# A perceiver layer's tail: one root for two norms, causal values straight to rows of queries, ranks from logits, other fillers

## What is computed

```python
def ffn(x):                         # x is layernorm(x2), eps 1e-5
    h = x + attention(rmsnorm(x, attn_norm_w), wq, wk, wv, wo)   # 16 heads of 16, rotary, causal
    return h + moe_ffn(rmsnorm(h, ffn_norm_w), router_w, w1, w2, w3)
def rmsnorm(x, w):
    return w * (x / sqrt(mean(x * x) + 1e-6))
def moe_ffn(x):                     # softmax, the best 2 of 8, renormalized
    topv, topi = top_k(softmax(x @ router_w), 2)
    combine = sum(topv / sum(topv) * one_hot(topi, 8))
    ye = (silu(x @ w1[e]) * (x @ w3[e])) @ w2[e]     # w1, w3: 256 x 512, w2: 512 x 256
    return sum over e of combine[e] * ye
out = x2 + ffn(layernorm(x2))
```

## Time and profile before

| | us |
|---|---|
| median of 3 runs | 535.7 (535.12 to 536.69) |
| the profiled execution | 535.16 |
| its span | 533.4 |
| PE busy in the span | 504.4 |
| DVE, ACT, POOL busy | 386.6, 346.4, 90.0 |

### The profile page before, as it was taken

How to read it: one execution, slowest core, us unless ns; L and a number is a source line. 1 busy time by engine, 2 the same in 40 slices (tenths; PEclk the granted TensorE clock), 3 DMA queues, 4 the chain that set the end, 5 groups by cost and what they waited for, 6 DMA issues and landing times.

```text
span 533.4 us, 19592 instructions
## 1 busy us (share of the span) xinstructions
PE 504.4 (95%) x8408; PEld 459.6 (86%) x8408; DVE 386.6 (72%) x712; ACT 346.4 (65%) x688; POOL 90.0 (17%) x75
## 2 busy tenths in 40 slices
PE   7898999999999999999999999999989989775997
PEld 7888899999999999999999999999877878564886
DVE  5488877777877777787787877787774347938574
ACT  3422687787778878878788787877766720162663
POOL 6761101111111110110110111110000000052000
PEclk9999999999999999999999999999999999869899
DMA  6554544343344434434434344432380079900000
GB/s 200 163 170 150 162 146 140 121 141 125 123 156 148 133 126 138 148 117 160 132 127 144 119 150 137 147 107 91 132 279 4 3 250 377 320 1 1 2 0 10
DMA packets 44630, 70.65 MB, mean 132 GB/s; under 512 B 6784, under 2 KB 15104, under 8 KB 44416
## 3 DMA queue, kind: packets, MB, share of 16 engines
q1 hardware_dynamic: 44304, 69.02, 39.0%
q10 hardware_dynamic: 240, 0.39, 0.3%
HBM read 30.53 MB, written 0.13 MB: 57 GB/s over the span
## 4 chain that ended last, share of the span: by engine, by line
PE 86%; DVE 9%; ACT 2%; issue 1%; POOL 0%; DMA 0%; SPq 0%; DVEq 0%; ACTq 0%
PE weighted L763 17%; PE scores L746 15%; PE bank L642 13%; PE bank L624 13%; PE maxima L669 11%; PE scores L1043 3%; PE maxima L1027 2%; DVE stepmax L1140 2%; PE scores L771 2%; PE bank L1027 2%; PE scores L792 1%; PE bank L571 1%; DVE stepmax L1132 1%; PE bank L591 1%; PE scores L1036 1%
## 5 line engine op out<-in xcount | busy, mean ns | idle before, releaser
L1140 DVE TENSOR_REDUCE stepmax<-maxima 128x2 f32<-128x512 f32 x344 | 225.5, 688 | 73.6 <-PE maxima L669 68.8
L437 ACT ACTIVATE probs<-scores 128x512 f32<-128x512 f32 x376 | 204.1, 596 | 74.1 <-PE scores L746 73.5
L624 PE MATMUL bank<-cparts,wk 64*128 64x256 f32 x1104 | 176.7, 287 | 1.7 <-DVE kst L1123 1.7
L642 PE MATMUL bank<-wv,cparts 64*128 64x256 f32 x1104 | 171.0, 287 | 0.4
L624 PEld LDWEIGHTS bank<-cparts,wk 64*128 64x128 f32 x1104 | 145.5, 187 | 2.6 <-DVE kst L1123 2.6
L642 PEld LDWEIGHTS bank<-wv,cparts 64*128 64x128 f32 x1104 | 145.5, 186 | 1.5 <-PE bank L642 1.5
L746 PE MATMUL scores<-qmat,kT 64*128 64x128 f32 x1504 | 112.9, 265 | 1.3 <-DMA qmat<-maxT 0.6
L669 PE MATMUL maxima<-kT,qM 64*128 64x256 f32 x688 | 111.6, 305 | 1.5 <-DVE stepmax L1140 1.3
L351 POOL TENSOR_TENSOR cparts<-ctxT,cparts 128x512 fp32r<-128x512 f32 x49 | 62.9, 1283 | 285.2 <-ACT cparts L397 285.2
L746 PEld LDWEIGHTS scores<-qmat,kT 64*128 64x128 f32 x1504 | 103.4, 188 | 3.8 <-ACT probs L437 1.7
L763 PE MATMUL weighted<-probs,val 128*17 128x128 f32 x3136 | 96.5, 273 | 0.0
(11 more groups left out here) (224 smaller groups left out, 424.9 us busy)
## 6 DMA issues: line engine op xcount, KB each, us to landing
kT<-kst SPq DMA_DIRECT2D x291, 128.0 KB, 2.6
ctxT<-in_ctxT SPq DMA_DIRECT2D x49, 256.0 KB, 3.2
w<-in_w SPq DMA_DIRECT2D x24, 512.0 KB, 10.1
bias<-in_biases SPq DMA_DIRECT2D x1, 1024.0 KB, 7.4
kT<-kst ACTq DMA_DIRECT2D x3, 128.0 KB, 3.2
qmat<-maxT SPq DMA_DIRECT2D x24, 8.0 KB
w_xk<-in_w_xk SPq DMA_DIRECT2D x1, 256.0 KB, 3.0
w_xq<-in_w_xq SPq DMA_DIRECT2D x1, 256.0 KB, 3.6
```

Source lines behind the costliest of these rows:

```text
L437: act.activation(probs[k % PROBS][:, :, :], late_bank[score_banks(k - q % 2)[q % 2]][:, :].rearrange("p (h q) -> p h q", q=P), ACT.Exp).th ...
L624: last = pe.matmul(k_bank[:, cols], wk[rows, pw, c, t * P:(t + 1) * P], cparts[n % 2][rows, pc, c, :], start=not swapped and i == 0, stop= ...
L642: last = pe.matmul(v_bank[:, cols], cparts[n % 2][rows, pc, c, j * P:(j + 1) * P], wv[rows, pw, c, :], start=not swapped and i == 0, stop= ...
L1140: dve.tensor_reduce(heads[:, 2 * m:2 * m + 2], bank[:, :].rearrange("p (i k) -> p i k", i=2), AX_X, ALU.max).then_inc(S["mx_read"], 1)
```

## The change

It touches only what comes after the keys' loop.

1. One root: the variance of the layernorm's result is v / (v + eps), so the product of both roots is the root of v (1 + 1e-6) + 1e-5 x 1e-6. `c_scale` is now made from that at once. `ln_root` is still needed for the residual `xl`; it and `xl` are made later, after DVE's copies to `pT`.
2. Causal values: each head is one product with `pT` as the stationary operand and the 17 columns of `vaug` moving (`causal_values`). `oT`, its copy and the four turns back are gone. DVE copies three groups to `pT` and ACT one.
3. Ranks: the comparisons read the scaled logits (`lg`) in place of the softmax; the first sum, reciprocal and product are gone, and the exponential goes to its own place.
4. ACT makes the high parts of the first two experts before it copies the queries, and POOL waits for `kbd` before the low parts.
5. Fillers: 8 for 6 before the turn of the queries, 6 new behind the scores, 3 after each of the first two groups' turns (`B[3]`), 10 before the first expert's turn. The sum of `hres` and `x2` moves behind the first gate.

```diff
@@ POOL
+            pool.wait_ge(S["dve_c_kbd"], 2 * DC)
             for e in range(2):
@@ ACT
+            act.wait_ge(S["experts_loaded"], 1)
+            highs(0, 0)
+            highs(1, 1)
             act.wait_ge(S["pe_c_qkT"], 2)
...
-            for g in (1, 3):
-                act.wait_ge(S["pe_c_pT"], g + 1)
-                act.activation(pT[:, GH * g:GH * (g + 1), :],
-                               B[g][:, :].rearrange("p (h q) -> p h q", q=P), ACT.Copy).then_inc(S["act_c_pT"], 1)
...
-            act.wait_ge(S["experts_loaded"], 1)
-            highs(0, 0)
-            highs(1, 1)
+            act.wait_ge(S["pe_c_pT"], GROUPS)
+            act.activation(pT[:, GH * (GROUPS - 1):H, :], B[GROUPS - 1][:, :].rearrange("p (h q) -> p h q", q=P), ACT.Copy
+                           ).then_inc(S["act_c_pT"], 1)
             act.wait_ge(S["dve_m_sub"], 1)
-            act.activation(small[:, 8:16], small[:, 8:16], ACT.Exp).then_inc(S["act_m_exp"], 1)
+            act.activation(small[:, 8:16], small[:, 192:200], ACT.Exp).then_inc(S["act_m_exp"], 1)
@@ PE
-            keep_busy(6)
+            keep_busy(8)
             pe.wait_ge(S["dve_c_qk"], 1)
...
+            keep_busy(6, B[3])
+            def causal_values(g):
+                if g < GROUPS - 1:
+                    pe.wait_ge(S["dve_c_pT"], g + 1)
+                else:
+                    pe.wait_ge(S["act_c_pT"], 1)
+                for h in range(GH * g, GH * (g + 1)):
+                    last = pe.matmul(B[5][:, 2 * HD * h:2 * HD * h + VW], pT[:, h, :], vaug[:, h, :], start=True, stop=True)
+                return last
...
-            pe.wait_ge(S["dve_c_pT"], 2)
-            pe.wait_ge(S["act_c_pT"], 2)
-            for g in range(GROUPS):
-                for r in range(GH):
-                    last = pe.matmul(B[4][32 * r:32 * r + VW, g * P:(g + 1) * P], vaug[:, GH * g + r, :],
-                                     pT[:, GH * g + r, :], start=True, stop=True)
-            last.then_inc(S["pe_c_pv"], 1)
-            pe.wait_ge(S["dve_c_oT"], 1)
-            for g in range(GROUPS):
-                last = pe.transpose(B[5][:, g * P:(g + 1) * P], oT[:, g, :], ident)
+                if g < 2:
+                    keep_busy(3, B[3])
+                elif g == 2:
+                    causal_values(0)
+            for g in range(1, GROUPS):
+                last = causal_values(g)
             last.then_inc(S["pe_c_o"], 1)
...
             up(0, 1, 0)
+            keep_busy(10)
             turn(0, 0)
@@ DVE
-            variance()
-            root_guess(ln_var, ln_root)
+            dve.tensor_scalar(rms_half, var, -0.5 * (1.0 + EPS_RMS), -0.5 * EPS_LN * EPS_RMS, ALU.mult, ALU.add)
+            link(dve.tensor_scalar(rms_var, var, 1.0 + EPS_RMS, EPS_LN * EPS_RMS, ALU.mult, ALU.add))
+            root_guess(rms_var, c_scale)
             turned(xnT, B[0], "pe_c_xnT", "dve_c_xnT")
-            root_steps(ln_half, ln_root, ln_tmp)
-            link(dve.tensor_scalar(square, ln_root, ln_root, var, ALU.mult, ALU.mult))
-            dve.tensor_scalar(rms_half, square, EPS_RMS, -0.5, ALU.add, ALU.mult)
-            link(dve.tensor_scalar(rms_var, square, EPS_RMS, None, ALU.add))
-            root_guess(rms_var, rms_root)
-            root_steps(rms_half, rms_root, rms_tmp)
-            link(dve.tensor_scalar(c_scale, rms_root, ln_root, None, ALU.mult))
+            root_steps(rms_half, c_scale, rms_tmp)
...
-            for g in (0, 2):
+            for g in range(GROUPS - 1):
                 dve.wait_ge(S["pe_c_pT"], g + 1)
...
-            dve.wait_ge(S["pe_c_pv"], 1)
-            dve.tensor_copy(oT[:, :, :], B[4][:, :].rearrange("p (g q) -> p g q", q=P)).then_inc(S["dve_c_oT"], 1)
+            variance()
+            root_guess(ln_var, ln_root)
+            root_steps(ln_half, ln_root, ln_tmp)
+            dve.tensor_scalar(xl[:, :], x2[:, :], mean, ln_root, ALU.subtract, ALU.mult)
...
-            link(dve.tensor_tensor(hres[:, :], hres[:, :], x2[:, :], ALU.add))
             dve.wait_ge(S["pe_m_logits"], 1)
...
-            dve.wait_ge(S["act_m_exp"], 1)
-            pr = small[:, 16:24]
-            link(dve.tensor_reduce(small[:, 1:2], small[:, 8:16], AX_X, ALU.add))
-            link(dve.reciprocal(small[:, 2:3], small[:, 1:2]))
-            link(dve.tensor_scalar(pr, small[:, 8:16], small[:, 2:3], None, ALU.mult))
...
-            dve.tensor_tensor(big, over_heads(pr, E), per_head(pr, E), ALU.is_gt)
+            dve.tensor_tensor(big, over_heads(lg, E), per_head(lg, E), ALU.is_gt)
...
-            link(dve.scalar_tensor_tensor(small[:, 32:40], small[:, 24:32], 1.5, pr, ALU.is_lt, ALU.mult))
+            dve.wait_ge(S["act_m_exp"], 1)
+            link(dve.scalar_tensor_tensor(small[:, 32:40], small[:, 24:32], 1.5, ex, ALU.is_lt, ALU.mult))
...
             gated(0, 0, False)
+            link(dve.tensor_tensor(hres[:, :], hres[:, :], x2[:, :], ALU.add))
             gated(1, 1)
```

More of the change, by code:

```diff
@@ L495, in _, with highs @@
             act.activation(tb[:, D:2 * D], tb[:, D:2 * D], ACT.Exp, scale=-1.0).then_inc(S["act_a_exp"], 1)
+            def highs(e, i):
+                for which in range(2):
+                    for c in range(DC):
+                        last = act.activation(high13[:, i, which, c, :], w13[which][:, e, c, :], ACT.Copy)
+                    last.then_inc(S["act_m_high"], 1)
+            act.wait_ge(S["experts_loaded"], 1)
+            highs(0, 0)
+            highs(1, 1)
             act.wait_ge(S["pe_c_qkT"], 2)
@@ L505, in _ @@
                 last.then_inc(S["act_c_exp"], 1)
-            for g in (1, 3):
-                act.wait_ge(S["pe_c_pT"], g + 1)
-                act.activation(pT[:, GH * g:GH * (g + 1), :],
-                               B[g][:, :].rearrange("p (h q) -> p h q", q=P), ACT.Copy).then_inc(S["act_c_pT"], 1)
-            def highs(e, i):
-                for which in range(2):
-                    for c in range(DC):
-                        last = act.activation(high13[:, i, which, c, :], w13[which][:, e, c, :], ACT.Copy)
-                    last.then_inc(S["act_m_high"], 1)
-            act.wait_ge(S["experts_loaded"], 1)
-            highs(0, 0)
-            highs(1, 1)
+            act.wait_ge(S["pe_c_pT"], GROUPS)
+            act.activation(pT[:, GH * (GROUPS - 1):H, :], B[GROUPS - 1][:, :].rearrange("p (h q) -> p h q", q=P), ACT.Copy
+                           ).then_inc(S["act_c_pT"], 1)
             act.wait_ge(S["dve_m_sub"], 1)
-            act.activation(small[:, 8:16], small[:, 8:16], ACT.Exp).then_inc(S["act_m_exp"], 1)
+            act.activation(small[:, 8:16], small[:, 192:200], ACT.Exp).then_inc(S["act_m_exp"], 1)
             act.wait_ge(S["dve_m_root"], 1)
@@ L766, in weighted_values, with keep_busy @@
                 last.then_inc(S["pv_done"], 1)
-            def keep_busy(n):
+            def keep_busy(n, bank=B[6]):
                 for _ in range(n):
-                    pe.matmul(B[6][:, 0:P], ident, ident, start=True, stop=True)
+                    pe.matmul(bank[:, 0:P], ident, ident, start=True, stop=True)
             def turn_part(b):
@@ L1320, in _ @@
             dve.tensor_scalar(vaug[:, :, 0:HD], B[2][:, 0:D].rearrange("p (h d) -> p h d", d=HD), c_scale, None, ALU.mult)
-            dve.tensor_scalar(xl[:, :], x2[:, :], mean, ln_root, ALU.subtract, ALU.mult)
             dve.wait_ge(S["pe_c_qkT"], 1)
@@ L1384, in _ @@
             link(dve.tensor_reduce(small[:, 0:1], B[7][:, 0:E], AX_X, ALU.max))
[L1385 removed]
+            lg, ex = small[:, 192:200], small[:, 8:16]
+            dve.tensor_scalar(lg, B[7][:, 0:E], small[:, 0:1], m_scale[:, :], ALU.subtract, ALU.mult
                               ).then_inc(S["dve_m_sub"], 1)
[L1387 to L1391 removed]
+            dve.wait_ge(S["dve_m_sub"], 1)
             big = small[:, 64:128].rearrange("p (a b) -> p a b", b=E)
             same = small[:, 128:192].rearrange("p (a b) -> p a b", b=E)
[L1395 to L1396 removed]
+            dve.tensor_tensor(big, over_heads(lg, E), per_head(lg, E), ALU.is_gt)
+            link(dve.tensor_tensor(same, over_heads(lg, E), per_head(lg, E), ALU.is_equal))
             link(dve.tensor_tensor(same, same, const[:, C_LT:C_LT + E * E].rearrange("p (a b) -> p a b", b=E),
```

7 lines of the change are left out of this document (2 added, 5 removed).

## The result

The changed kernel takes **531.9 us** (median of 4 runs, 531.47 to 531.95) against 536.12 in the same runs: a ratio of 0.9932, interval [0.9912, 0.9953]. A second set of runs gave 531.86 us and 0.9949 [0.9917, 0.9981]. It is faster, as forecast, but by 4.2 us, where 529.1 us would have been 7.0 less than this median; and it lies 0.3 us above the top of the range. Between the two profiled executions, on which the sum was made, it is less still: the spans are 533.4 and 530.1 us, 3.3 us where the sum said 6.25.

What follows compares the result with a forecast made beforehand. PE bounds the keys' loop, but the tail is one dependence between DVE, ACT and PE. Gains of 1.0, 2.4, 1.15, 1.2 and 1.8 against delays of 0.7 and 0.6 gave -6.25 us: 529.1 us forecast, range 526.9 to 531.6.

Steps and rivals of the forecast that it cites:

- I take +0.7: Start of causal scores: PE waits for ACT's queries' copy behind the highs; +0.7 us, bounds 0 and +1.0.
- All of the 2.1 us is gone: Before the scores: the 2.1 us gained by making one root is lost to ACT's later queries' copy.
- +0.6: Under DVE's masks and maxima: the four `minus_max` wait for POOL's low products; +0.6 us, at most 1.3.
- fill a cadence of 1.3 us per group nearly: Around the causal values: fillers keep PE busy, so full clock is assumed from there; values take 3.4 us, -2.4.
- -1.15: From the values to `hres`: fillers at full clock, the first three under DVE's two operations; -1.15 us.
- (C): Rival: PE's clock stays low through the values, 3.2 us more there and 1.15 behind; 533.4 us, 12%.
- L1366, -1.0: DVE product with both inputs in SBUF runs alone, no longer beside POOL's products; -1.0 us.
- Ranks and the residual sum, -1.2: Way to the experts: residual sum leaves the path, -0.45, and ranks skip the exponential, -0.75; together -1.2 us.
- Ten fillers, -1.8: Before the first expert's turn: ten fillers hold the clock, 5.39 us of work takes 3.56; -1.8 us.
- Rival (A): Neither delay comes: POOL doesn't touch `minus_max` and the clock falls late; -7.55 us, 527.6 us, 15%.
- (B): Rival: the root's gain survives if `experts_loaded` comes by 453 us; -9.7 us, 525.5 us, 3%.
- (D): Rival: POOL's eight products hold up all twelve DVE operations between 461 and 471 us; 538.6 us, 3%.

Runs made afterwards that it cites:

- the second profile: The changed kernel run again with nothing altered: 531.86 us, 0.9949 of the kernel before.
- queries first: Changed kernel with ACT copying the turned queries before it makes the high parts: 530.86 us, 0.9926 of the kernel before.
- combined kernel without wide values: Changed kernel with ACT copying the queries ahead of the highs and row maxima in PSUM, values still moving 17 columns: 528.12 us, 0.9869 of the kernel before.
- the combined one: Changed kernel with queries copied ahead of the highs, row maxima in PSUM and up to 68 moved columns for the values: 525.17 us, 0.9818 of the kernel before.

## Why the prediction was wrong

The direction, the hold at the scores and the single gains of the values, of L1366 and of the ranks were right; the gain was taken about 3 us too large. By the steps of the sum:

- **"PE can't start the scores before 462.25 ... I take +0.7."** Right in this profile: PE started at 462.46, the first mask came 0.61 us later than before. In the second profile it was 1.31, above my upper bound of 1.0. What I left out is the second product: at the lower clock it takes 1.7 us, more than DVE's turn, and costs 0.36 more. The experiment with the queries first shows the hold itself: 3.5 us at the first mask. **"All of the 2.1 us is gone"** is true of the first mask only: with two roots the kernel takes 2.2 us more.
- **POOL, "+0.6", with "the later three would wait little (0.1 each)".** Mis-sized: the waits were 0.37 and 1.11 us, 1.5 in all, beyond my upper bound of 1.3 (1.1 in the second profile), and 2.2 and 2.5 us in two other kernels. DVE's turn of 1.31 us and POOL's of 1.23 don't run in step; one slides past the other, and a product that comes just behind the start of POOL's next waits for all of it.
- **"The fillers ... fill a cadence of 1.3 us per group nearly, which is why I take full clock from here on": the step that failed.** The values themselves ran at full clock and took what I had worked out (3.44 against 3.4). But their 16 products, PE busy throughout, let the clock fall behind them, and the **-1.15** for the way to `hres` became +0.14. I had the mechanism among the rivals (C), at 12%, and had it begin with the values; it comes at their end here, and with the values in the kernel with the queries first. The same products with more moved columns kept the clock, so in this kernel it was the columns.
- **L1366, -1.0**: -1.02. **Ranks and the residual sum, -1.2**: -0.95. The next small product, L1392, started 0.39 us behind L1390, 0.21 before; why is open. **Ten fillers, -1.8**: -1.62; the new rounds are 3.78 us where I took 3.56 from a later round, whose first product follows without a gap. The ranks and the moved residual sum were not run by themselves; their gain is read from the two profiles.
- Rival (A), at 527.6, described what is had when both holds are taken away, not what happens by itself. (B) did not happen, `experts_loaded` came at 457.8. (D) did not happen: masks and maxima took 0.67 to 0.69 us beside POOL.

Summed over the profiled executions: 0.27 (second product, less what the first mask fell short of 0.7), 0.86 (POOL), 1.29 (clock behind the values), 0.25 (gates), 0.18 (ten fillers) and 0.14 of start, with nothing for the values and L1366: 3.0 us, the whole of the miss between the profiles. The forecast was also not the sum's: 6.25 us off the median of 535.7 gives 529.45, and I wrote 529.1.

## What to carry to other kernels

A gain upstream is worth what the next wait lets through, so look at what each engine does first in its new order: one reorder of ACT held the first mask up by 3.5 us. Keep an engine's small SBUF to SBUF products away from POOL's long ones, or give them a PSUM operand. And read the granted clock, not only PE's busy time: here it fell during or just behind products with 17 moved columns, with PE busy, and not with 68 columns, which took no more time.

## What the runs showed of the hardware

- Products of 128 loaded and 17 moved columns take 0.22 us each at full clock (12 in 2.6 us), the same as with 68 moved columns. In the combined kernel without wide values the granted clock fell among them (470.5) though PE had been busy for 10.37 of the 10.5 us before; with 68 it stayed at 1.00.
- A DVE product from SBUF to SBUF waits for POOL's running product also where it has only 4 columns (up to 1.27 in place of 0.15 us); one with a single column ran undisturbed beside it (0.14), and with 256 columns it took 1.03 in place of 0.41.
- The times of one kernel differ by some 2 us with the beginning. The first 20 us of the kernel before, and of the combined one in a profile whose statistics of `x2` came 2.1 us later:

```profile
14.00:16.00 2.00, 2.00 (x21) 1.00 1.00 260
...
14.00:16.00 2.00, 2.00 (x12) 0.50 0.92 265
```

In the second the clock was at its lower level from 13.6 us, and all that followed came later. Five of the thirteen profiles had it, the same five whose statistics of `x2` begin at 452.5 to 452.9 and not at 450.1 to 451.1. In these five PE came back from a wait of 1.93 or 1.94 us for POOL's `cparts` at 13.2 to 13.6 us; in the other eight the wait was 1.5 to 1.94 us and PE was back by 12.3 to 13.1. So the length of the wait does not tell them apart; what makes the clock fall in some stays open. None of the edits touches that place, and fillers for this wait were not tried.
